# Scores per head on 32 array rows, in a three-step round of a gated attention kernel

## The chip, the cores and the metric

One Trainium2 chip, one core. The metric is the device time of one execution in microseconds (us). Engines are named as the profile names them: PE is TensorE (matrix products, with PEld for its weight loads), DVE is VectorE, ACT is ScalarE, POOL is GpSimd, SP is SyncE, which here only issues transfers.

## The reference

Eight sequences of 512 tokens with 256 features go through a gated linear attention against a context and then through a mixture of experts. The part around the change, for one sequence, with 8 heads of 32 features:

```python
qk = jnp.einsum('hsd,htd->hst', qh, kh) / np.sqrt(DH)
C = qk * D_mat                                   # D_mat = exp(log_D - max), causal
normalizer = jnp.maximum(jnp.abs(C.sum(axis=-1, keepdims=True)), jnp.exp(-max_log_D))
h = jnp.einsum('hst,htd->hsd', C / (normalizer + EPS), vh)
```

`q` is the layer-normed token, `k` and `v` are both the context. After a layer norm and a residual, each token goes through 2 shared experts (hidden 1024) and the best 2 of 8 routed experts, and all is summed.

## The kernel before, in words

The first part of the kernel handles attention, routing and the shared experts; the second, from about 765 us on, handles the routed experts and is not touched.

A sequence is cut in J = 4 blocks of 128 tokens. What lies before a block enters through a `state` (one product of 132 columns for each half of the heads), what lies in it is computed directly, in a round j for each block:

1. exponents: for each half g of the heads (4 heads), a matmul with `identb` and `causal`, and one with `exp_lhs` and `exp_rhs` (56 rows) on top, 512 columns each, into banks 0 and 1;
2. scores: for each half, one fp32 matmul of 512 columns into banks 2 and 3. Its stationary side is the context block, all 128 features of the half; its moving side is `qmask`, which holds the queries four times, each time with all but one head's 32 features at zero (`headmask`). So a contraction over 128 rows gives each head's own product. `qmask` is filled by DVE (g = 0, L698) and POOL (g = 1, L475), four instructions each for a sequence;
3. `decay` = exp of banks 0 and 1 by ACT (L567); `ct` = scores x scale x `decay` by DVE (L767), one instruction for each half;
4. state products into bank 0 (L1066) and value products (L1071), eight fp32 matmuls, each head's beside the next in banks 2 and 3; `hn` by DVE (L775 to L783) adds them up.

An fp32 matmul appears in the trace as two records. banks(b, j) are PSUM banks 0 to 3, except that sequence 0 takes banks 4 to 7 for odd j.

Each engine follows one list of steps written by hand: `START` before the first pass, `FIRST`, then `ORDER` for each pass, `ORDER_6` for the last but one. In pass b, `U` is a unit of the shared experts of sequence b (16 in all: up product, Gelu and cast on ACT, low part on DVE, down product of an earlier unit), digits and S, T, V, W, X are steps of `back(b+1)` (the attention of the next sequence: the digits are its rounds), F, G, M, R, C, c are steps of `front(b+2)` (norm, transposes, gates, the operands of the exponents), A, Q, B, D, E are routing, H hands the tokens over to the shared experts (`xhs` on ACT, `xls` on DVE), L is the last down product and Y the `finish` of sequence b-1, P the base of the output. Each engine does its own share of a step and goes on; between engines there are only semaphores. An engine that waits in one step so holds back all its later ones.

In a pass before, round 0 had no unit between its two steps, rounds 1 to 3 one each, with others between rounds; PE issued exponents and scores together in the first step of a round, and waited for `decay` and `ct` in the second.

## Time and profile before

| | |
|---|---|
| median of 3 runs | 1243.25 us (1241.1 to 1245.12) |
| profiled execution | 1241.27 us, its span 1239.5 us |
| PE busy | 1137.4 us (92%), weight loads 996.7 us |
| DVE busy | 919.4 us (74%) |
| ACT busy | 837.6 us (68%) |
| POOL busy | 341.8 us (28%) |
| mean granted TensorE clock | 0.964 of full speed |

The span runs from the first to the last instruction; the execution's time is 1.8 us more. Busy shares are means over the whole span. PE's matmuls overlap in the records: the distance from one start to the next says what a matmul really costs in a row of them, not its own duration.

### The profile page before, as it was taken

To read this page: it belongs to the slowest core of one execution; us is meant where nothing else is said; L and a number is where in the kernel's file an instruction comes from. 1 tells how busy PE (TensorE), PEld (TensorE's weight loads), DVE (VectorE), ACT (ScalarE), POOL (GpSimd) and SP (SyncE) were. 2 spreads that over 40 slices of the span, in tenths; PEclk is the share of its full clock that TensorE was granted. 3 is DMA by queue.
4 is the path that set the end of the run, shared out by engine and by line. 5 is a ranking of instruction groups with operands and counts; after the bars stand their busy time and mean duration, and the time that the engine had idled before them with its cause. 6 is when DMAs were issued, how large, how long until landed. Compare 5 with 4: busy or idle time off the path is not lost. (4 is left out here: it accounts for less than half of the span.)

```text
span 1239.5 us, 21821 instructions
## 1 busy us (share of the span) xinstructions
PE 1137.4 (92%) x7861; PEld 996.7 (80%) x7861; DVE 919.4 (74%) x2215; ACT 837.6 (68%) x1441; POOL 341.8 (28%) x319
## 2 busy tenths in 40 slices
PE   2748999999989999989989897999999999999996
PEld 1436776886777777777868787999999999999996
DVE  5885696686777777866955564888888888888883
ACT  3526556566476556565664353999999999999994
POOL 7121221510510412313113020233333233333333
PEclk9776999999999999999999898999999999999998
DMA  6110011111010100110001035788888888888872
GB/s 197 34 35 17 34 36 35 36 35 35 35 52 23 65 27 32 46 35 35 19 17 44 1 121 170 219 220 233 239 212 232 244 208 232 244 209 230 246 186 27
DMA packets 141692, 136.17 MB, mean 110 GB/s; under 512 B 48599, under 2 KB 127585, under 8 KB 141585
## 3 DMA queue, kind: packets, MB, share of 16 engines
q1 hardware_dynamic: 122948, 111.68, 28.6%
q0 software_dynamic: 14304, 18.75, 9.2%
q10 hardware_dynamic: 4332, 4.34, 1.0%
q8 instruction: 63, 1.03, 0.3%
q14 instruction: 45, 0.36, 0.1%
HBM read 109.42 MB, written 25.33 MB: 109 GB/s over the span
## 5 line engine op out<-in xcount | busy, mean ns | idle before, releaser
L1358 DVE TENSOR_TENSOR wlo<-big,whi 128x512 fp32r<-128x512 f32 x312 | 219.9, 716 | 21.8 <-ACT whi L1311 14.4
L1311 ACT CAST whi<-big 128x512 fp32r<-128x512 f32 x312 | 191.2, 615 | 6.5 <-PEq L420 5.1
L590 ACT ACTIVATE shared_hraw<-bank,b1s 128x512 f32<-128x512 f32 x128 | 88.1, 688 | 153.9 <-PE bank L1119 153.6
L1283 PE MATMUL bank<-xhi,whi 128*128 128x256 f32 x624 | 175.6, 281 | 6.3 <-DVE xlo L1372 5.1
L1261 PE MATMUL bank<-whi,hhi 128*128 128x256 f32 x624 | 178.1, 285 | 0.0
L1283 PE MATMUL bank<-xhi,wlo 128*128 128x256 f32 x624 | 174.5, 280 | 0.0
L1261 PE MATMUL bank<-wlo,hhi 128*128 128x256 f32 x624 | 174.4, 280 | 0.0
L1261 PE MATMUL bank<-whi,hlo 128*128 128x256 f32 x624 | 174.4, 280 | 0.0
L1283 PE MATMUL bank<-xlo,whi 128*128 128x256 f32 x624 | 174.3, 279 | 0.0
L1333 ACT ACTIVATE hraw<-bank,b 128x256 f32<-128x256 f32 x312 | 147.9, 474 | 36.2 <-PE bank L1283 35.3
L835 DVE TENSOR_TENSOR shared_hlo<-shared_hraw,shared_hhi 128x512 fp32r<-128x512 f32 x128 | 93.1, 731 | 96.4 <-ACT shared_hhi L593 92.9
L495 POOL DMA_INDIRECT sorted_tokens<-rowbuf,slots x64 | 66.7, 1042 | 322.5 <-DVEq L911 305.5
L1102 PE MATMUL bank<-whs,shared_hhi 128*128 128x256 f32 x512 | 150.2, 293 | 3.8 <-DVE shared_hlo L835 3.8
L1402 DVE TENSOR_TENSOR hlo<-hraw,hhi 128x512 fp32r<-128x512 f32 x156 | 108.0, 693 | 55.3 <-ACT hhi L1338 49.7
L1102 PE MATMUL bank<-whs,shared_hlo 128*128 128x256 f32 x512 | 146.0, 285 | 0.0
L1102 PE MATMUL bank<-wls,shared_hhi 128*128 128x256 f32 x512 | 145.9, 285 | 0.0
L1436 POOL DMA_INDIRECT out_dram<-yt,token x78 | 135.4, 1736 | 29.3 <-issue 18.7
L1119 PE MATMUL bank<-xhs,whs 128*128 128x512 f32 x256 | 118.1, 461 | 9.5 <-ACT shared_hraw L590 5.9
L1283 PEld LDWEIGHTS bank<-xhi,whi 128*128 128x128 f32 x624 | 118.9, 190 | 6.7 <-POOL xhi L1425 5.3
L1283 PEld LDWEIGHTS bank<-xlo,whi 128*128 128x128 f32 x624 | 119.0, 191 | 0.0
L1283 PEld LDWEIGHTS bank<-xhi,wlo 128*128 128x128 f32 x624 | 118.2, 189 | 0.0
L1261 PEld LDWEIGHTS bank<-whi,hhi 128*128 128x128 f32 x624 | 117.7, 189 | 0.0
(275 smaller groups left out, 2634.6 us busy)
## 6 DMA issues: line engine op xcount, KB each, us to landing
big<-in_L_ffn_W_r_dram SPq DMA_DIRECT2D x78, 1024.0 KB, 7.4
qcT<-sorted_tokens SPq DMA_DIRECT2D x39, 260.0 KB, 2.9
xb<-in_x_dram SPq DMA_DIRECT2D x8, 512.0 KB, 4.6
cb<-in_ctx_dram SPq DMA_DIRECT2D x8, 512.0 KB, 3.5
xr<-in_x_dram SPq DMA_DIRECT2D x8, 512.0 KB, 3.5
out_dram<-base ACTq DMA_DIRECT2D x8, 512.0 KB, 2.9
sorted_tokens<-chunk SPq DMA_DIRECT2D x9, 260.0 KB, 3.4
out_dram<-yt,token POOLq DMA_INDIRECT x78, 4.0
```

The source lines that it names most:

```text
L495: nc.gpsimd.indirect_dma_start(out=xs_dram, out_offset=bass.IndirectOffsetOnAxis(ap=slots[:, k, j:j + 1], axis=0), in_=rowbuf[:, j, :], in ...
L590: nc.scalar.activation(hraw[:, k % NHB, :], up_bank[k % 2][:, :], ACT.Gelu, bias=b1s[:, k // M, k % M:k % M + 1]).then_inc(gelu_done, 1)
L835: tt(hlo[:, k % NHB, :], hraw[:, k % NHB, :], hhi[:, k % NHB, :].bitcast(fp32), ALU.subtract).then_inc(hlo_ready, 1)
L1102: last = mm(down_bank[j // 2][:, (j % 2) * D:(j % 2 + 1) * D], h[:, k % NHB, j * P:(j + 1) * P], w[:, e, wsl], start=k == 0 and t == 0 and ...
L1119: last = mm(up_bank[k % 2][:, :], w[:, e, wsl], x_[:, c, :], start=c == 0 and t == 0, stop=c == KD - 1 and t == 2)
L1261: last = nc.tensor.matmul(y_bank[i][j * D // 512][:, (j * D) % 512:(j * D) % 512 + D], l[:, h, j * P:(j + 1) * P], w[i][:, wsl], start=m = ...
L1283: last = nc.tensor.matmul(ub[:, 0:T], w[i][:, wsl], x_[i][:, k, :], start=k == 0 and t == 0, stop=k == KD - 1 and t == 2)
L1311: nc.scalar.copy(whi[i][:, psl], raw[i][:, psl]).then_inc(t_whi, 1)
L1333: nc.scalar.activation(hraw[:, m % NHB, :], psum[m % NU][:, 0:T], ACT.Gelu, bias=b1[i][:, m:m + 1]).then_inc(t_gelu, 1)
L1358: nc.vector.tensor_tensor(wlo[i][:, psl], raw[i][:, psl], whi[i][:, psl].bitcast(fp32), ALU.subtract).then_inc(t_wlo, 1)
L1402: nc.vector.tensor_tensor(hlo[:, h - 1:h + 1, :], hraw[:, h - 1:h + 1, :], hhi[:, h - 1:h + 1, :].bitcast(fp32), ALU.subtract).then_inc(t_ ...
L1436: nc.gpsimd.indirect_dma_start(out=out_r, out_offset=bass.IndirectOffsetOnAxis(ap=token[n % NG][:, j:j + 1], axis=0), in_=yt[i][:, j, :], ...
```

## The change

The masks `headmask` and `qmask` go, with their fills on DVE and POOL (an unused tensor `space` keeps the layout). A head's scores are now a matmul of their own: 32 rows of the array, those on which the head's features lie, and 128 columns. Head r of each half writes to bank r, half g to columns g x 128 onwards, so all four banks are used, and the scores overwrite the exponents, which ACT must have read (`decay_ready`). `ct` takes four instructions, one for each bank. State products go to bank 2, value products to bank 3, one head's 99 columns overlapping the next head's, and `hn` adds them in one instruction. Of the exponents, both `causal` matmuls now come before both `exp_lhs` ones. A round has three steps instead of two (exponents; scores; products), and the lists place units between all of them; H comes before round 0. The wait for `counts_read` before round 3 is gone.

```diff
-        START = "f f f f w w w f f w w f f S w w w 0 w w 0 w w 1 w w g 1 w 2 w g 2 3 3 g T T T V V g g V W h g u g u X g".split()
-        FIRST = "S 0 U 0 1 A U 1 F U Q 2 U F 2 B U P 3 U 3 D G M T E U T U T R V U V U V U R U W U X C U c".split()
-        ORDER = "S 0 L H Y 0 U 1 A U 1 F U Q 2 U F 2 B U P 3 U 3 D U G M T E U T U Z T U Z R V U V U V U R U W U X C U c".split()
-        ORDER_6 = "S 0 L H Y 0 U 1 A U 1 U Q 2 U 2 B U P 3 U 3 D U T E U T T U V U V V U W U X U U U U".split()
+        START = "f f f f w w w f f w w f f S w w w 0 w w 0 0 w w 1 w w 1 g 1 w 2 2 w g 2 3 3 3 g T T T V V g g V W h g u g u X g".split()
+        FIRST = "S 0 U 0 U 0 1 A U 1 U 1 2 F U 2 Q U 2 3 F U 3 P U 3 B U D G M T E T U T R V U V U V R U W X C U c".split()
+        ORDER = "S H 0 L 0 Y U 0 1 U 1 A U 1 2 F U 2 Q U 2 3 F U 3 P U 3 B U D G M T E U T U Z T U Z R V U V V U R U W U X C U c".split()
+        ORDER_6 = "S H 0 L 0 Y U 0 1 U 1 A U 1 2 U 2 Q U 2 3 U 3 P U 3 B U D T E U T T U V V V U W U X U U U U".split()
...
-                    for r in range(HG):
-                        last = nc.gpsimd.tensor_scalar(qmask[:, 1, r, :], qcT[:, 1, :], headmask[:, r:r + 1], None,
-                                                       ALU.mult)
-                    last.then_inc(qmask_pool, 1)
...
-                    for r in range(HG):
-                        last = ts(qmask[:, 0, r, :], qcT[:, 0, :], headmask[:, r:r + 1], None, ALU.mult)
-                    last.then_inc(qmask_dve, 1)
...
-                        for g in range(KD):
-                            last = stt(ct[:, g * HG:(g + 1) * HG, :],
-                                       banks(b, j)[2 + g][:, :].rearrange("p (h s) -> p h s", s=P), SCALE,
-                                       decay[:, g * HG:(g + 1) * HG, :], ALU.mult, ALU.mult)
+                        for r in range(HG):
+                            last = stt(ct[:, :, :].rearrange("p (g r) s -> p g r s", r=HG)[:, :, r, :],
+                                       banks(b, j)[r][:, 0:KD * P].rearrange("p (g s) -> p g s", s=P), SCALE,
+                                       decay[:, :, :].rearrange("p (g r) s -> p g r s", r=HG)[:, :, r, :], ALU.mult, ALU.mult)
...
+                    def exponents(j):
                         cj = slice(j * P, (j + 1) * P)
-                        if b > 0 and j > 0:
-                            pe.wait_ge(hn_ready, J * b + j)
                         if b == 0 and j > 1:
                             pe.wait_ge(hn_ready, j - 1)
-                        if j == 3 and b > 0:
-                            pe.wait_ge(counts_read, b)
-
                         for g in range(KD):
                             mm(banks(b, j)[g][:, :], identb[:, :], causal[:, :].unsqueeze(1).to_broadcast([P, HG, P]),
                                start=True, stop=False)
+                        for g in range(KD):
                             last = mm(banks(b, j)[g][:, :], exp_lhs[:, cj],
                                       exp_rhs[:, j, g * HG:(g + 1) * HG, :].rearrange("p h s -> p (h s)"),
                                       start=False, stop=True)
                         last.then_inc(exp_done, 1)
+
+                    def scores(j):
+                        cj = slice(j * P, (j + 1) * P)
+                        pe.wait_ge(decay_ready, J * b + j + 1)
                         if j == 0:
                             pe.wait_ge(state_ready, b + 1)
-                            pe.wait_ge(qmask_dve, b + 1)
-                            pe.wait_ge(qmask_pool, b + 1)
+                        elif b > 0:
+                            pe.wait_ge(hn_ready, J * b + j)
                         for g in range(KD):
-                            last = mm(banks(b, j)[2 + g][:, :], qcT[:, KD + g, cj], qmask[:, g, :, cj], start=True, stop=True)
+                            for r in range(HG):
+                                last = mm(banks(b, j)[r][:, g * P:(g + 1) * P], qcT[r * DH:(r + 1) * DH, KD + g, cj],
+                                          qcT[r * DH:(r + 1) * DH, g, cj], start=True, stop=True)
                         last.then_inc(score_done, 1)
...
+                    for j in range(J):
+                        if j == 0:
+                            pe.wait_ge(lhs_ready, b + 1)
+                            pe.wait_ge(exp_act, b + 1)
...
+                        if b > 0 or j == 0:
+                            exponents(j)
+                        yield
+                        if b == 0 and j + 1 < J:
+                            exponents(j + 1)
+                        scores(j)
                         yield
                         cj = slice(j * P, (j + 1) * P)
-                        pe.wait_ge(decay_ready, J * b + j + 1)
+                        pe.wait_ge(ct_ready, J * b + j + 1)
                         if j > 0:
                             for g in range(KD):
-                                mm(banks(b, j)[0][:, g * HW:(g + 1) * HW], qcT[:, g, cj], state[:, g, j - 1, :],
+                                mm(banks(b, j)[2][:, g * HW:(g + 1) * HW], qcT[:, g, cj], state[:, g, j - 1, :],
                                    start=True, stop=True)
-                        pe.wait_ge(ct_ready, J * b + j + 1)
                         vflat = vaug[:, j, :, :].rearrange("p h e -> p (h e)")
                         for h in range(NH):
-                            last = mm(banks(b, j)[2 + h // HG][:, (h % HG) * PW:(h % HG + 1) * PW], ct[:, h, :],
+                            last = mm(banks(b, j)[3][:, h * VW:h * VW + PW], ct[:, h, :],
                                       vflat[:, h * VW:h * VW + PW], start=True, stop=True)
```

## Rows read from the trace of the kernel before

**Rows 1.** Busy time by stretch: from:to, length, each engine's busy us, clock, DMA
```profile
...
43.20:69.40 26.20, 22.48 (x110) 14.13 (x108) 19.83 (x52) 8.71 (x16) 0.00 (x0) 0.96 0.13 41
...
111.70:151.00 39.30, 38.53 (x227) 28.94 (x226) 24.01 (x74) 21.30 (x28) 5.72 (x6) 1.00 0.08 29
...
196.00:234.40 38.40, 37.51 (x214) 27.48 (x215) 25.12 (x75) 23.35 (x30) 5.79 (x6) 1.00 0.13 43
234.40:282.20 47.80, 45.68 (x283) 38.62 (x280) 38.92 (x102) 29.16 (x43) 14.75 (x14) 0.96 0.10 33
```

**Rows 2.** What TensorE waited for, 110 to 680 us: total, times, longest
```profile
...
PE bank L1037 <- ACT big L555: 11.9, 6, 2.3
PE bank L1119 <- ACT shared_hraw L590: 4.8, 6, 0.8
PE bank L1071 <- DVE chunk L767: 4.0, 6, 0.7
```

**Rows 3.** Timeline of PE, round 1 of a pass: start us, us, instruction
```profile
...
203.96 0.39 PE L1037 MATMUL bank<-causal,identb 128*128 128x512 bf16 x1
...
205.25 1.99 PE L1048 MATMUL bank<-big,qcT 128*128 128x512 f32 x4
...
207.30 0.39 PE L1119 MATMUL bank<-xls,whs 128*128 128x512 f32 x1
207.53 0.39 PE L1119 MATMUL bank<-xhs,wls 128*128 128x512 f32 x1
```

**Rows 4.** Timeline of PE, end of round 2: state and value products
```profile
...
220.45 0.61 PE L1066 MATMUL bank<-state,qcT 128*128 128x132 f32 x4
220.90 1.92 PE L1071 MATMUL bank<-vaug,chunk 128*128 128x99 f32 x16
222.66 0.18 PE L1135 MATMUL bank<-sel,tri 128*128 128x32 bf16 x1
```

**Rows 5.** Timeline of PE: the first matmuls of two units in succession
```profile
...
244.21 0.40 PE L1119 MATMUL bank<-xhs,whs 128*128 128x512 f32 x1
...
247.04 0.40 PE L1119 MATMUL bank<-xhs,whs 128*128 128x512 f32 x1
```

**Rows 6.** Timeline of ACT at the start of a pass
```profile
...
195.85 1.28 ACT L567 ACT_TABLE_LOAD   x1
197.34 1.09 ACT L567 ACTIVATE chunk<-bank 128x512 f32<-128x512 f32 x2 [0.21 <-PE bank L1039]
198.32 1.05 ACT L629 CAST xhs<-unT 128x1024 fp32r<-128x1024 f32 x1
202.91 0.40 ACTq L597 DMA_DIRECT2D out_dram<-base  x1
...
204.63 0.69 ACT L590 ACTIVATE shared_hraw<-bank,b1s 128x512 f32<-128x512 f32 x1
205.35 0.62 ACT L593 CAST shared_hhi<-shared_hraw 128x512 fp32r<-128x512 f32 x1
```

**Rows 7.** Timeline of DVE: qmask beside POOL idle, ct, finish, qmask beside POOL
```profile
...
88.31 1.67 DVE L698 TENSOR_SCALAR big<-qcT,headmask 128x512 f32<-128x512 f32 x4
...
199.26 1.29 DVE L767 SCALAR_TENSOR_TENSOR chunk<-bank,chunk 128x512 f32<-128x512 f32 x2 [3.54 <-PE bank L1048]
...
201.60 1.28 DVE L842 TENSOR_TENSOR base<-base,bank 128x512 f32<-128x512 f32 x2
...
240.25 2.90 DVE L698 TENSOR_SCALAR big<-qcT,headmask 128x512 f32<-128x512 f32 x4 [1.90 <-ACT qcT L529]
```

**Rows 8.** Timeline of POOL: its half of qmask
```profile
...
73.88 6.29 POOL L475 TENSOR_SCALAR big<-qcT,headmask 128x512 f32<-128x512 f32 x4
```

**Rows 9.** Timeline of PE: a pass's first exponents, last products, next pass's exponents
```profile
...
195.97 0.38 PE L1037 MATMUL bank<-causal,identb 128*128 128x512 bf16 x1 [1.34 <-ACT big L555]
...
232.48 1.92 PE L1071 MATMUL bank<-vaug,chunk 128*128 128x99 f32 x16
...
282.24 0.38 PE L1037 MATMUL bank<-causal,identb 128*128 128x512 bf16 x1 [1.36 <-ACT big L555]
```

More of the change, by code:

```diff
@@ L116, in xattn_moe_kernel @@
         take_two = A("take_two", [KE, 1])
-        headmask = A("headmask", [P, HG])
+        A("space", [P, HG])
         blockmask = A("blockmask", [P, HG, VW])
@@ L144, in xattn_moe_kernel @@
         qn = A("qn", [P, J, D])
-        qmask = big[0][:, :].rearrange("p (g r s) -> p g r s", g=KD, r=HG)
         norm_x, norm_u = ((A(f"bn6_{n}", [P, J, 6]), A(f"mv_{n}", [P, J, 2]), A(f"nw_{n}", [P, 5, J])) for n in "xu")
@@ L240, in _ @@
                 nc.gpsimd.memset(causal[:, :], 0.0)
-                nc.gpsimd.memset(headmask[:, :], 1.0)
                 nc.gpsimd.memset(exp_lhs[:, :], 0.0)
@@ L763, in back @@
                     for j in range(J):
+                        yield
                         dve.wait_ge(score_done, J * b + j + 1)
                         dve.wait_ge(decay_ready, J * b + j + 1)
-                        for g in range(KD):
-                            last = stt(ct[:, g * HG:(g + 1) * HG, :],
-                                       banks(b, j)[2 + g][:, :].rearrange("p (h s) -> p h s", s=P), SCALE,
-                                       decay[:, g * HG:(g + 1) * HG, :], ALU.mult, ALU.mult)
+                        for r in range(HG):
+                            last = stt(ct[:, :, :].rearrange("p (g r) s -> p g r s", r=HG)[:, :, r, :],
+                                       banks(b, j)[r][:, 0:KD * P].rearrange("p (g s) -> p g s", s=P), SCALE,
+                                       decay[:, :, :].rearrange("p (g r) s -> p g r s", r=HG)[:, :, r, :], ALU.mult, ALU.mult)
                         last.then_inc(ct_ready, 1)
@@ L772, in back @@
                         dve.wait_ge(pv_done, J * b + j + 1)
+                        pvv = banks(b, j)[3][:, 0:NH * VW].rearrange("p (h e) -> p h e", e=VW)
                         if j > 0:
                             rr = eexp[:, NW + (j - 1) * NH:NW + j * NH].unsqueeze(2).to_broadcast([P, NH, VW])
-                            own.done(tt(hn[:, j, :, :], banks(b, j)[0][:, 0:NH * VW].rearrange("p (h e) -> p h e", e=VW),
+                            own.done(tt(hn[:, j, :, :], banks(b, j)[2][:, 0:NH * VW].rearrange("p (h e) -> p h e", e=VW),
                                         rr, ALU.mult))
-                        for g in range(KD):
-                            pvv = banks(b, j)[2 + g][:, 0:HG * PW].rearrange("p (h e) -> p h e", e=PW)[:, :, 0:VW]
-                            dst = hn[:, j, g * HG:(g + 1) * HG, :]
-                            if j > 0:
-                                last = tt(dst, dst, pvv, ALU.add)
-                            else:
-                                last = nc.vector.tensor_copy(dst, pvv)
-                        last.then_inc(hn_ready, 1)
+                            tt(hn[:, j, :, :], hn[:, j, :, :], pvv, ALU.add).then_inc(hn_ready, 1)
+                        else:
+                            nc.vector.tensor_copy(hn[:, j, :, :], pvv).then_inc(hn_ready, 1)
                         yield
@@ L1026, in back @@
                     yield
-                    def scores(j):
+                    def exponents(j):
                         cj = slice(j * P, (j + 1) * P)
-                        if b > 0 and j > 0:
-                            pe.wait_ge(hn_ready, J * b + j)
                         if b == 0 and j > 1:
                             pe.wait_ge(hn_ready, j - 1)
-                        if j == 3 and b > 0:
-                            pe.wait_ge(counts_read, b)
                         for g in range(KD):
@@ L1052, in back @@
-                    pe.wait_ge(exp_act, b + 1)
-                    if b == 0:
-                        pe.wait_ge(s_const, 6)
-                        scores(0)
-                    for j in range(J):
-                        if b > 0:
-                            scores(j)
-                        elif j + 1 < J:
-                            scores(j + 1)
+                    for j in range(J):
+                        if j == 0:
+                            pe.wait_ge(lhs_ready, b + 1)
+                            pe.wait_ge(exp_act, b + 1)
+                            if b == 0:
+                                pe.wait_ge(s_const, 6)
+                        if b > 0 or j == 0:
+                            exponents(j)
+                        yield
+                        if b == 0 and j + 1 < J:
+                            exponents(j + 1)
+                        scores(j)
```

6 lines of the change are left out of this document (removed).

## The prediction

> **What bounds the kernel now.** I read the page first: TensorE is busy for 92% of the span, but a busy PE is not a PE at its peak, so I went on to the busy time by stretch. From 680 us on (the last pass and the routed experts) no changed instruction runs. The change lives in seven stretches of rounds that run beside units of the shared experts, and in one without units (43.2 to 69.4). In the pass that begins at 196 PE is busy 37.5 of 38.4 us over the rounds and 45.7 of 47.8 us over the rest, while DVE is busy 25.1 and 38.9, ACT 23.4 and 29.2 [rows 1]. The waits confirm it: between 110 and 680 PE waits for ACT's `exp_rhs` 11.9 us in all, then for two things of 4.8 and 4.0 us [rows 2]. So a pass is a queue of PE work in a written order. A microsecond taken off PE is a microsecond won, unless what PE waits for next comes later than that. Both halves of this sentence must be priced.
>
> **PE work of a round, before.** From the first exponent matmul to the scores are 1.29 us: four matmuls of 512 columns at 0.32 each, though 512 columns of a unit's matmul pass in 0.23 (207.30 to 207.53) [rows 3]. The difference, 0.09, comes with each change between 128 and 56 rows. The scores start at 205.25, and the unit behind them reaches its pace of 0.23 at 207.30, so its first matmul really ran from 207.07: the scores cost 1.82. State products cost 0.45 (220.45 to 220.90), value products 1.76 (to 222.66) for sixteen records, 0.11 each [rows 4]. A whole unit is 2.83, from 244.21 to 247.04 [rows 5].
>
> **The same, after.** Exponents: two `causal` matmuls together, then two `exp_lhs`: two changes of rows instead of four, 2 x 0.23 + 2 x 0.32 = 1.10, so 0.19 saved. State and value products keep their shapes, banks apart. The scores become 8 fp32 matmuls of 128 columns, 16 records, with as many columns in all as now (2 x 512). The trace has no four matmuls on different array rows, so this is the unknown price. *Upper bound*: no overlap, each record as long as one of the value products, which also load 128 weight columns: 16 x 0.11 = 1.76, with 0.18 for going to 32 rows and back 1.94. *Lower bound*: four at once, 0.44 + 0.18 = 0.62. I take a value between: matmuls start in order and the second record of a head must wait for its own first, but the next head's first can run beside it, so 9 steps of 0.11 + 0.18 = 1.17, or 0.65 saved. I lean to overlap because the records sit on disjoint rows and write four different banks.
>
> The Trainium skill ("TensorE: Matmul & The Clock Gate", Part 3) gives a measured 3.07 times for four row tiles of 512 columns; by it the scores would cost 1.76 / 3.07 + 0.18 = 0.75, an estimate. Its section on LDWEIGHTS says the opposite for loads: their time goes with the columns, not the rows, which would hold all 16 loads at full price; the value products' 0.11 at only 99 moving columns agree [rows 4]. By that the scores would be 1.94. No row here decides between them.
>
> **DVE, POOL, ACT.** DVE loses `qmask` (2.90 us per sequence beside POOL's own) [rows 7]. `ct` goes from two instructions (1.29 the pair [rows 7]) to four of half the size; I put 1.45 for the four, 0.15 more for the additional starts. `hn` adds once instead of twice, a hair less. POOL loses 6.29 us of `qmask` [rows 8]. None of this is on PE's path where PE bounds; it only gives slack. Once it counts: from 70 to 88 PE waits for DVE (the chain up to the tokens' transposes), POOL's `qmask` runs from 73.9 to 80.2, and DVE's own took 2.90 beside POOL against 1.67 without [rows 7, 8]. I put 1.5 us for that.
>
> **The new dependence.** Scores now overwrite the exponents' banks, so they wait for ACT's `decay` of the same round; before they ran right behind the exponents. The order puts a unit (2.83) between. Walk one pass, with T the start of exponents 0:
> - Exponents end at T+1.1, the late unit (1.4) at 2.5. ACT first copies `xhs` (1.05, now ahead), loads its table (1.28) and does two exponentials (1.09) [rows 6]; it is free at about T-0.1, so `decay` 0 is there at 3.2. PE waits 0.7; scores 3.2 to 4.4; unit 0 (no down part) to 5.8; `ct` 0 ready 6.1; value products to 7.9; exponents 1 to 9.0; unit 1 to 10.4.
> - Now ACT is late. It waits for `finish` on DVE, which sits behind `ct` 0 (1.28 more [rows 7]: 7.4), issues a DMA (0.4), loads the Gelu table (1.28), does Gelu and the cast (1.3 [rows 6]): 10.4. Only then table and `decay` 1: 12.8. PE stands still for 2.4 us. Behind the waiting scores are unit 2 and everything else on PE. Before, the same `decay` 1 delay was covered by a unit whose work came behind the already issued scores, and cost 0.7 (the L1071 wait, [rows 2]).
> - Scores to 14.0; unit 2 to 16.8. `ct` 1 stands in DVE's queue behind the low part of unit 1, whose Gelu stands behind `decay` 1 and two table loads: 17.5, so PE waits 0.9. Value products to 19.9.
> - Rounds 2 and 3: each exponents 1.1, unit 2.83, scores 1.17, unit 2.83, products 2.2 = 10.1, without waits: `decay` needs 1.1 after its exponents, `ct` comes 1.8 to 2.9 after the scores, even behind a front step of DVE. End at T+40.0.
>
> Before, with T at 195.97, round 3's products began at 232.48 and ended 1.76 later, T+38.3, with six units done [rows 9]; after, seven are done. Gain of a pass: 38.3 + 2.83 - 40.0 = 1.1. The rest of the pass loses one unit of PE work and stays PE's: DVE's chain there sheds `qmask` and one low part, 3.6 together, more than the 2.83 PE sheds. The last piece (rows, exponents' operands, the 2 us wait for `exp_rhs`) is the same chain and stays. Six such passes: 6.6 us.
>
> The first pass (111.7 to 151.0 over its rounds [rows 1], six units there) has no `finish`, `late` or `xhs` ahead: no 2.4 us stall. After: 4 x 1.10 + 4 x 1.17 + 4 x 1.76 + 3 x 0.45 + 8 x 2.83 = 40.1 against 39.3 with two units (5.66) fewer: 4.9 gained. Two units leave its second part, where DVE then comes close to PE; I keep 3.5.
>
> The rounds without units (43.2 to 69.4 [rows 1]): `ct` j, `decay` j+1, scores j+1, `ct` j+1 becomes one chain, some 1.2 us longer a round than the old one without scores in it, but a round takes 6.6 now and DVE's front step lies there anyway; I put +1.7 and cancel it with POOL's relief (-1.5).
>
> **Sum.** 1239.5 - 6.6 - 3.5 = 1229.4 us of span; the profiled execution took 1241.3, 1.8 more than its span, and the median of the runs is 1243.25, 2.0 above that. So 1233.
>
> **Rivals.**
> - *Row tiles don't overlap* (scores 1.94). Per pass, T+42.2 instead of 40.0: 1.1 slower than before; six passes +6.6; the first gains 1.8; the rounds without units +3 on their chain. Sum +8: 1251, slower. For it: weight loads set the pace of the value products. Against: disjoint rows. It decides from a score price of about 1.7. Chance 0.22.
> - *The stall does not appear or something covers it, PE stays the bound*: 28 rounds x (0.65 + 0.19) = 23.5, with 1 to 2 of the old waits: 1218. For it: PE's largest waits sum to 21 us in 570 [rows 2]. Against: ACT's order is strict and each piece of it is in the rows. Chance 0.15.
> - *Overlap works but waits eat all*: A is now apart from `decay`, so ACT reloads tables twice more a pass (2.6 us); if that reaches PE once in a pass, the 1.1 is gone and only the first pass is left, 1240 to 1244. Chance 0.13.
> - Forecast, 1226 to 1239: 0.50.
>
> What a measurement can tell from no change is 0.3%, 3.7 us. Faster 0.65, same 0.13, slower 0.22. For 8 in 10 the range takes in most of both outer rivals, with 1 to 2 us beyond their values, since each is itself a sum of bounds: 1216 to 1253.
>
> **What would show it.** After: from the first score matmul to the unit's pace about 1.2 us (1.9 if serial); exponents 1.1; PE waits of some 2.4 us before round 1's scores on ACT's `decay`, in six passes; round 3's products done 40 us after exponents 0; passes of 85 instead of 86.3 us (195.97 to 282.24 [rows 9]). The forecast is wrong if scores cost over 1.7, or if rounds 2 and 3 wait for `ct`, or if the second part of a pass doesn't shorten by a unit.

## The result, and the profile after

| | before | after |
|---|---|---|
| median | 1243.05 us (1241.10 to 1245.12, 4 runs) | 1261.72 us (1256.77 to 1262.06, 4 runs) |
| span of the profiled execution | 1239.5 us | 1259.9 us |
| mean granted TensorE clock | 0.964 | 0.935 |

The ratio is 1.0141 (95% interval 1.0111 to 1.0171): slower by 18.7 us. I had forecast 1233, with 1216 to 1253. Both the sign and the range are missed.

The head of the page of the changed kernel (its span, then busy us, share and instructions of each engine):

```profile
span 1259.9 us, 22586 instructions
...
PE 1126.2 (89%) x8245; PEld 1007.5 (80%) x8245; DVE 895.7 (71%) x2215; ACT 853.8 (68%) x1453; POOL 287.0 (23%) x284
```

PE, DVE and POOL all do less than before, as they were to, and yet the span is 20.4 us longer. So the question isn't what the new instructions cost but where engines stand. Busy time and granted clock by stretch of the changed kernel (columns as in [rows 1]: the first rounds; the first pass's rounds; the rounds and the rest of a later pass):

```profile
41.40:78.80 37.40, 28.44 (x159) 21.15 (x157) 20.49 (x57) 8.83 (x16) 0.00 (x0) 0.55 0.10 29
117.30:156.40 39.10, 39.10 (x301) 32.52 (x300) 24.47 (x76) 24.98 (x33) 0.00 (x0) 1.00 0.05 15
288.60:328.10 39.50, 36.89 (x279) 29.83 (x279) 24.98 (x77) 27.39 (x34) 0.00 (x0) 0.96 0.07 25
328.10:376.20 48.10, 43.41 (x270) 36.46 (x268) 35.87 (x101) 27.92 (x41) 13.62 (x15) 0.96 0.14 47
```

Against [rows 1]: the first rounds took 26.2 us and take 37.4, at a clock of 0.55 where it was 0.96. The rounds of a pass take about as long as they did, with a unit more in them. The rest of a pass takes 48.1 where it took 47.8, though it has a unit less: PE is busy 43.4 us there instead of 45.7, and idle 4.7 instead of 2.1.

I cut both traces at each pass's first exponent matmul, at the end of its last value product, and at the first matmul of the routed experts (all in us; "half clock" is the time that the granted clock was at its lower level, 1.2 GHz, from the first rounds' start to the first pass, and from there to the end of the last rounds). "Last" is the last pass that has rounds; its rest, up to the routed part, also holds the pass of the last sequence, which has none:

| | first rounds | rest | rounds, pass 1 / 2 to 6 / last | rest, pass 1 / 2 to 6 / last | routed part starts | half clock, first rounds / passes |
|---|---|---|---|---|---|---|
| before | 26.4 | 42.1 | 39.3 / 38.4 to 39.8 / 39.3 | 44.9 / 47.8 / 103.2 | 771.1 | 34.3 / 13.7 |
| after | 37.4 | 38.5 | 39.3 / 39.1 to 40.3 / 39.3 | 44.7 / 48.2 / 111.1 | 791.8 | 58.8 / 48.0 |

So the 20.4 us are: 5.6 up to the start of pass 1 (111.7 to 117.3), -0.2 in pass 1, 7.3 in the five later ones (432.7 us became 440.0), 7.9 in the rest of the last pass, and -0.2 in the routed part.

What PE waited for from 100 to 700 us in the changed kernel (columns as in [rows 2]):

```profile
PE bank L1033 <- ACT chunk L556: 14.0, 9, 2.1
PE bank L1016 <- ACT big L544: 9.8, 6, 2.3
PE bank L991 <- DVE rows L701: 8.8, 7, 1.8
PE bank L1106 <- ACT shared_hraw L580: 4.8, 6, 0.8
PE bank L974 <- ACT frow L596: 4.5, 6, 0.8
```

The first row is the forecast stall: scores that wait for `decay`. The third is not in [rows 2] and not in the forecast: the transposes of `rows`, right behind the gates' part, wait for DVE. Both are seen in the timeline. PE of the changed kernel, the start of a pass:

```profile
288.64 0.59 PE L1016 MATMUL bank<-causal,identb 128*128 128x512 bf16 x2 [1.89 <-ACT big L544]
289.17 0.60 PE L1019 MATMUL bank<-big,exp_lhs 56*128 56x512 bf16 x2
...
291.88 0.73 PE L1033 MATMUL bank<-qcT 32*128 32x128 f32 x16 [0.49 <-ACT chunk L556]
292.54 0.50 PE L1106 MATMUL bank<-xhs,whs 128*128 128x512 f32 x1
292.88 0.39 PE L1106 MATMUL bank<-xls,whs 128*128 128x512 f32 x1
293.11 0.39 PE L1106 MATMUL bank<-xhs,wls 128*128 128x512 f32 x1
...
296.01 0.59 PE L1016 MATMUL bank<-causal,identb 128*128 128x512 bf16 x2
296.54 0.60 PE L1019 MATMUL bank<-big,exp_lhs 56*128 56x512 bf16 x2
297.07 0.50 PE L1106 MATMUL bank<-xhs,whs 128*128 128x512 f32 x1
...
300.81 0.73 PE L1033 MATMUL bank<-qcT 32*128 32x128 f32 x16 [2.08 <-ACT chunk L556]
301.47 0.52 PE L1106 MATMUL bank<-xhs,whs 128*128 128x512 f32 x1
301.81 0.61 PE L1106 MATMUL bank<-xls,whs 128*128 128x512 f32 x1
302.21 0.63 PE L1106 MATMUL bank<-xhs,wls 128*128 128x512 f32 x1
302.64 0.63 PE L1106 MATMUL bank<-xhs,whs 128*128 128x512 f32 x1
```

Scores take 0.66 (291.88 to 292.54) and the unit behind them starts 0.11 slower than its pace of 0.23 (0.34 to the next): 0.77 in all. The four exponent matmuls take 1.06 (296.01 to 297.07). The stalls are 0.49 and 2.08. Behind the second one the unit's matmuls follow each other at 0.40 to 0.43 instead of 0.23: the granted clock has fallen to its lower level. It does so right behind this stall in four of the six passes that have it, not in the other two.

In the rest of the same pass, PE and DVE of the changed kernel:

```profile
364.83 0.47 PE L991 MATMUL bank<-ident,rows 72*128 72x72 f32 x4 [1.24 <-DVE rows L701]
...
376.18 0.59 PE L1016 MATMUL bank<-causal,identb 128*128 128x512 bf16 x2 [1.90 <-ACT big L544]
```

```profile
335.09 0.21 DVE L773 SCALAR_TENSOR_TENSOR rnorm<-hn 128x32 f32<-128x32 f32 x1 [3.26 <-ACT qcT L518]
```

DVE stands 3.26 us at the wait that `qmask` needed and that nothing needs now (`qcT_ready`). That was my first suspect for the late `rows`; it was the wrong one.

### The profile page after: what moved, and what is told of

It is laid out like the page before. It is cut to its first block and busy times, and to the rows that moved or that the text cites. A ratio compares the mean times of both kernels' runs of the same rounds, so it can differ in the third digit from the quotient of the medians.

```text
span 1259.9 us, 22586 instructions
## 1 busy us (share of the span) xinstructions
PE 1126.2 (89%) x8245; PEld 1007.5 (80%) x8245; DVE 895.7 (71%) x2215; ACT 853.8 (68%) x1453; POOL 287.0 (23%) x284
## 5 line engine op out<-in xcount | busy, mean ns | idle before, releaser
L1345 DVE TENSOR_TENSOR wlo<-big,whi 128x512 fp32r<-128x512 f32 x312 | 219.9, 716 | 26.2 <-ACT whi L1298 14.3
L1089 PE MATMUL bank<-wls,shared_hhi 128*128 128x256 f32 x512 | 150.3, 294 | 0.0
L1089 PE MATMUL bank<-whs,shared_hlo 128*128 128x256 f32 x512 | 150.0, 293 | 0.0
L1423 POOL DMA_INDIRECT out_dram<-yt,token x78 | 135.7, 1739 | 29.2 <-issue 18.7
L1106 PE MATMUL bank<-xhs,whs 128*128 128x512 f32 x256 | 114.9, 449 | 8.4 <-ACT shared_hraw L580 4.8
```

The source lines that it names most:

```text
L1089: last = mm(down_bank[j // 2][:, (j % 2) * D:(j % 2 + 1) * D], h[:, k % NHB, j * P:(j + 1) * P], w[:, e, wsl], start=k == 0 and t == 0 and ...
L1106: last = mm(up_bank[k % 2][:, :], w[:, e, wsl], x_[:, c, :], start=c == 0 and t == 0, stop=c == KD - 1 and t == 2)
L1345: nc.vector.tensor_tensor(wlo[i][:, psl], raw[i][:, psl], whi[i][:, psl].bitcast(fp32), ALU.subtract).then_inc(t_wlo, 1)
L1423: nc.gpsimd.indirect_dma_start(out=out_r, out_offset=bass.IndirectOffsetOnAxis(ap=token[n % NG][:, j:j + 1], axis=0), in_=yt[i][:, j, :], ...
```

## The experiments

Two theories, formed on the two traces. **Lists**: the new matmuls are as cheap as they look, and the time is lost where the lists now let engines wait (first rounds a serial chain, rounds' second stall, `rows`, the last pass's operands), so moving single steps gives it back. **Clock**: matmuls on 32 rows, or many short ones, pull the granted clock down; lists matter little, and only full rows would give the time back.

Each kernel is compared with before on its own chip. In two of the four series before itself took 1254 to 1255 us, on the other two 1241 to 1242, so ratios don't carry from one series to another; across series I compare the stretches of the table above, each from one trace of the kernel. The changed kernel itself ran only beside series 2 and in the first measurement, not on the chips of series 1 and 4.

**Series 1** (before 1254.48 us).

*full_rows*: scores on all 128 rows, 8 records of 256 columns instead of 16 of 128 (the queries are not masked: the attention values are not the reference's; the other work stands).

```diff
-                        for g in range(KD):
-                            for r in range(HG):
-                                last = mm(banks(b, j)[r][:, g * P:(g + 1) * P], qcT[r * DH:(r + 1) * DH, KD + g, cj],
-                                          qcT[r * DH:(r + 1) * DH, g, cj], start=True, stop=True)
+                        for r in range(HG):
+                            last = mm(banks(b, j)[r][:, 0:KD * P], qcT[:, KD + r % KD, cj],
+                                      qcT[:, 0:KD, cj], start=True, stop=True)
```

> The changed kernel with the scores on all 128 rows again: four fp32 matmuls of 256 columns for a round, as many columns in all as before the change, in the same four banks and at the same place of the round. The moving side is the unmasked queries, so the attention values are not the reference's; everything else is. Theory lists (the 32-row scores cost 0.75 us and are a gain; the loss comes from the step lists, which leave DVE and ACT late where PE used to be): scores 1.8 us instead of 0.75, so up to 1 us more in each of 28 rounds, partly in waits that are there anyway: 10 to 28 us slower than the changed kernel, 1272 to 1290. Theory clock (short 32-row matmuls make PE look idle and the granted clock falls, 165 us at half clock against 92 before): half-clock time goes back to about 100 us and the kernel is no slower than the changed one, at or under 1262.

Measured: 1282.99 us, ratio 1.0224 (1.0202 to 1.0247), span 1279.8. The rounds of a pass take 42.1 to 44.4 instead of 39.1 to 40.3. PE at the first scores of a pass:

```profile
294.06 1.99 PE L1032 MATMUL bank<-qcT 128*128 128x256 f32 x8 [0.50 <-ACT chunk L556]
295.70 0.58 PE L1105 MATMUL bank<-xhs,whs 128*128 128x512 f32 x1
```

1.64 us from start to start, with the same number of columns in all: on 32 rows it is 0.66. So row tiles do run beside each other. Nor do full rows keep the clock up in the passes: 51.6 us at the lower level, against 48.0. Only up to the first pass do they (34.2 against 58.8; the first rounds are 31.6 us long instead of 37.4).

*no_qct_wait*: DVE's useless wait taken out.

```diff
-                    dve.wait_ge(qcT_ready, J * b + J)
```

> The changed kernel without the wait of DVE for qcT_ready, which stood ahead of the qmask fills and was left when they went. In the trace DVE stands 3.3 us there in each pass before the normalisation chain, and PE later waits 1.2 us for rows. Theory lists: DVE's chain starts earlier, PE's wait for rows (8.8 us in all) goes: 5 to 9 us faster than the changed kernel, 1253 to 1257. Theory clock: within 2 us of it, since PE's waits there do not decide.

Measured: 1256.43 us, 1.0011 (0.9998 to 1.0024). The rest of pass 1 falls from 44.7 to 42.5; that of the five later ones stays at 48.1 to 48.2. So this wait is not what makes `rows` late there.

*scores_first*: in the first rounds, scores j are issued before exponents j+1.

```diff
+                        scores(j)
                         if b == 0 and j + 1 < J:
                             exponents(j + 1)
-                        scores(j)
```

> The changed kernel, where in the first sequence a round's scores are issued ahead of the next round's exponents instead of behind them. In the trace each of these rounds takes 10.4 us and is one chain (exponents, scores, ct, products, hn, next exponents), at half clock. Theory lists: the exponents (1 us, 1.9 at half clock) leave the chain three times: 3 to 6 us faster, 1256 to 1259, more if the clock then stays up. Theory clock (it falls because of the 32-row matmuls): rounds stay at half clock, 0 to 3 us faster.

Measured: 1255.50 us, 1.0001 (0.9981 to 1.0020). The first rounds take 31.7 instead of 37.4 us; their rest gives 1.7 of it back (40.2), and they began 2.5 us later in this execution, so pass 1 starts at 115.8 instead of 117.3.

*last_list*: the last pass follows the list `ORDER` of the kernel before (here `ORDER_7`), the others the new one.

```diff
-                for step in START if b < 0 else FIRST if b == 0 else ORDER_6 if b == B - 2 else ORDER:
+                for step in START if b < 0 else FIRST if b == 0 else ORDER_6 if b == B - 2 else ORDER_7 if b == B - 1 else ORDER:
```

> The changed kernel, whose last pass (units and routing of the last sequence, no rounds) follows the step list of the kernel before, so that routing comes after 4 units and not after 8. In the trace the loads for the routed experts are issued 18.8 us later than before while the units end 16.1 us later, and PE waits 9.7 us instead of 5.1 for the first routed tile. Theory lists: 4 to 5 us faster than the changed kernel, 1257. Theory clock: no change.

Measured: 1255.84 us, 1.0004 (0.9988 to 1.0020), span 1253.8. The rest of the last pass takes 104.4 instead of 111.1. How much of the 6.7 us is the edit's is not sure: the other kernels with the new list there, among them the changed kernel run again, took 107.6 to 109.9, so it is worth between 3 and 7 us. What DVE waits for there, after and in this kernel:

```profile
788.41 0.69 DVE L1345 TENSOR_TENSOR wlo<-big,whi 128x512 fp32r<-128x512 f32 x1 [7.83 <-DMA gr_col<-in_L_ffn_g_routed_dram]
```

```profile
780.71 0.69 DVE L1346 TENSOR_TENSOR wlo<-big,whi 128x512 fp32r<-128x512 f32 x1 [3.27 <-DMA gr_col<-in_L_ffn_g_routed_dram]
```

And what PE waits for from 600 to 800 us, after:

```profile
PE bank L1270 <- DVE xlo L1359: 9.7, 1, 9.7
PE bank L1067 <- DVE rowbuf L800: 8.8, 1, 8.8
```

Before had 5.1 us in the place of the first row, and so has last_list. The second row is another matter: 8.8 us here, 3.1 before, and 9.3 in last_list. It stands in the rest behind the last rounds, which follows `ORDER_6`, and no edit of mine but late_finish's move of Y touches that list; what makes `rowbuf` late there I haven't tested. In the new list of the last sequence's pass seven units stand ahead of B and eight ahead of D, where there were four and six. So the last pass's routing is done later, and SP, which waits for it, issues the routed experts' loads 126.1 us after the pass's first exponents (767.41) instead of 120.0 (748.61).

**Series 2** (before 1241.03 us).

*changed_again*, the changed kernel unedited. 

> The changed kernel as it is, beside the runs that follow. In the last series the kernel before took 1254 instead of 1243 us, so a ratio is only sure beside the changed kernel on the same chip. Theory lists and theory clock both expect the ratio of the first measurement, 1.014; if the ratio is nearer 1.000, the last series' variants gained nothing and the machine decides about 1%.

Measured: 1260.72 us, 1.0135 (1.0100 to 1.0170): the result stands. Its rounds and middle passes agree with the first trace within 0.3 us; the rest of the last pass took 109.7 instead of 111.1, pass 1 began at 118.2 instead of 117.3, and 51.2 us of the passes were at half clock.

*before_again*, the kernel before unedited. 

> The kernel before as it is, for its profile beside the others. Expected: the passes of 86 us as before (rounds 38.3, rest 48.0), and any added time in the transfers of the routed experts or at the boundary ahead of them, not in the passes.

Measured, one execution: 1241.58 us, span 1239.5.

*three_fixes*: no_qct_wait, scores_first and last_list together. 

> The changed kernel with the three edits together: no wait of DVE for qcT_ready, scores ahead of the next exponents in the first sequence, and the last pass by the step list of before. Theory lists: the gains lie in different stretches and add up: 12 to 17 us faster than the changed kernel in the same series, which is about the kernel before. Theory clock: under 5 us.

Measured: 1249.26 us, 1.0064 (1.0047 to 1.0081). The first rounds 30.1, the rest of pass 1 42.5, that of the last 104.4. The edits add up: 5.1 (pass 1 starts at 112.2 instead of 117.3), 2.2 and 6.7 are 14.0, and the routed part starts 13.8 earlier, at 778.0 instead of 791.8. The medians differ by less, 11.5 us (1260.72 and 1249.26).

*exponents_only*: the kernel before, with only the exponents' order changed (both `causal`, then both `exp_lhs`).

```diff
                         for g in range(KD):
                             mm(banks(b, j)[g][:, :], identb[:, :], causal[:, :].unsqueeze(1).to_broadcast([P, HG, P]),
                                start=True, stop=False)
+                        for g in range(KD):
                             last = mm(banks(b, j)[g][:, :], exp_lhs[:, cj],
```

> The kernel before with one part of the change alone: both causal matmuls of a round ahead of both exp_lhs ones. 0.19 us of PE saved in each of 28 rounds that PE bounds: up to 5 us faster than before, 0.4%; if waits take it back, 0.

Measured: 1241.39 us, 0.9989 (0.9976 to 1.0002): nothing that can be told from no change. The four matmuls take 1.07 us as forecast, and three of the five later passes' rounds are 0.6 us shorter (37.8). But the other two took 39.0 and 40.4, and the routed part starts at 770.8 against 771.1: the gain went to the clock, 27.3 us at the lower level in the passes instead of 13.7 (17.3 in before_again). The other executions bear it out: seven of ten had a mean granted clock of 0.958 or 0.959, where before has 0.962 to 0.966 on this chip, and the three at 0.962 to 0.965 took only 1237.2 to 1237.9 us.

**Series 3** (before 1242.24 us). Here the aim was the five middle passes.

*late_finish*: in the new list, `finish` (Y) goes from ahead of round 0's scores to behind round 1's exponents, so that ACT reaches `decay` 1 before it takes up the output (`ORDER_6` likewise).

```diff
-        ORDER = "S H 0 L 0 Y U 0 1 U 1 A U 1 2 F U 2 Q U 2 3 F U 3 P U 3 B U D G M T E U T U Z T U Z R V U V V U R U W U X C U c".split()
+        ORDER = "S H 0 L 0 U 0 1 Y U 1 A U 1 2 F U 2 Q U 2 3 F U 3 P U 3 B U D G M T E U T U Z T U Z R V U V V U R U W U X C U c".split()
```

> The changed kernel with Y (finish of the last sequence, on which ACT waits before it issues a transfer) behind the first exponents of round 1 instead of ahead of unit 0, in ORDER and ORDER_6. Theory lists: ACT no longer stands behind DVE there, decay 1 is ready before PE wants it, the 2.1 us stall of PE goes and the rounds of a pass fall from 39.4 to about 37.3: 10 to 13 us faster than the changed kernel. Theory clock: half-clock time in the passes (55 us) stays, and at most the 2.1 us themselves are saved; if the clock drops come from this stall, they go too and passes save up to 3 us each.

Measured: 1238.77 us, 0.9970 (0.9960 to 0.9980), span 1235.1. Rounds of the later passes 36.6 us each (the last 37.5) instead of 39.1 to 40.3. What PE waits for, 100 to 700 us:

```profile
PE bank L1067 <- DVE rowbuf L800: 9.3, 1, 9.3
PE bank L991 <- DVE rows L701: 8.8, 7, 1.8
PE bank L1016 <- ACT big L544: 7.3, 6, 1.9
...
PE bank L1054 <- DVE chunk L755: 3.8, 6, 0.7
PE bank L1033 <- ACT chunk L556: 2.5, 5, 0.5
```

`decay` costs 2.5 us in all instead of 14.0; what comes in its place (L1054, the forecast's wait for `ct` 1) is 3.8 (1.9 before the edit). This edit of one letter is worth 24.9 us of the routed part's start (791.8 to 766.9): 16.1 in the five middle passes, 5.1 in the last, and 3.6 ahead of pass 1, where nothing was edited. Those 3.6 are chance: the first rounds took 32.3 us in this execution and 37.4 to 37.7 in the six others with the same code there.

*unit_behind_gates*: one unit moved from between B and D, ahead of the gates, to the Vs behind them.

```diff
-        ORDER = "S H 0 L 0 Y U 0 1 U 1 A U 1 2 F U 2 Q U 2 3 F U 3 P U 3 B U D G M T E U T U Z T U Z R V U V V U R U W U X C U c".split()
+        ORDER = "S H 0 L 0 Y U 0 1 U 1 A U 1 2 F U 2 Q U 2 3 F U 3 P U 3 B D G M T E U T U Z T U Z R V U V U V U R U W U X C U c".split()
```

> The changed kernel with one unit of ORDER moved from between B and D to behind the gates (R V U V U V U R). In the trace PE does 4 units between the gates and the rows, before it did 5, and waits 1.2 us there for rows, whose chain (gates, ACT's logarithm and tables, Gelus, DVE's low parts and scans) starts at the gates. Theory lists: the unit fills that wait, 1 to 1.5 us of each of five passes: 5 to 7 us faster. If instead DVE is late for another reason, the wait stays and nothing changes.

Measured: 1264.08 us, 1.0166 (1.0147 to 1.0184), not faster as I expected but 3.4 us above the changed kernel on the same chip. The rest of a later pass takes 47.4 to 49.1, once 52.2, instead of 48.2. The wait for `rows` is gone from the five passes, a new one is there (PE, 100 to 700 us):

```profile
PE bank L1033 <- ACT chunk L556: 14.1, 10, 2.1
PE bank L1016 <- ACT big L544: 10.3, 6, 2.3
PE bank L1133 <- DVEq L887: 5.8, 5, 1.2
```

The unit between B and D had covered DVE's part of the routing; without it D's transposes wait 1.2 us in each of five passes.

*all_lists*: three_fixes, late_finish and unit_behind_gates together. 

> The changed kernel with all edits so far: no wait for qcT_ready, scores ahead of the next exponents in the first sequence, the last pass by the list of before, Y behind exponents 1, and the unit behind the gates. Theory lists: the three earlier edits gave 11.5 us, the other two give 15 more: 1232 to 1238 where before is 1241, faster than both kernels. Theory clock: no faster than 1245.

Measured: 1235.49 us, 0.9946 (0.9930 to 0.9961). Rounds 36.6 (once 37.5), first rounds 30.3, last rest 106.0.

*first_full_rows*: the full-row scores of full_rows in the first rounds alone (there the values are not the reference's).

```diff
-                        for g in range(KD):
+                        for g in range(KD if b > 0 else 0):
...
+                        for r in range(HG if b == 0 else 0):
+                            last = mm(banks(b, j)[r][:, 0:KD * P], qcT[:, KD + r % KD, cj],
+                                      qcT[:, 0:KD, cj], start=True, stop=True)
```

> The changed kernel with scores on all 128 rows for the first sequence only (unmasked queries, so its attention values are not the reference's), all others on 32 rows. Theory clock: with full-row matmuls the clock in the first sequence's rounds stays up longer, as with full rows everywhere (rounds 31.6 instead of 37.4 us, half clock until pass 1 35 us instead of 64): 4 to 6 us faster than the changed kernel although its matmuls are longer. Theory lists alone: 2 to 4 us slower than it, since the chain of a round grows by 1 us.

Measured: 1256.84 us, 1.0111 (1.0094 to 1.0129). First rounds 31.4 instead of 37.4, their rest 40.2 instead of 38.5, half-clock time up to pass 1 34.1 instead of 58.8 us.

**Series 4** (before 1254.80 us).

*unit_from_ahead*: late_finish, and one unit moved from the stretch just behind G M T E (ahead of the `rows`' transposes) to the Vs; the units from B to E stay.

```diff
-        ORDER = "S H 0 L 0 Y U 0 1 U 1 A U 1 2 F U 2 Q U 2 3 F U 3 P U 3 B U D G M T E U T U Z T U Z R V U V V U R U W U X C U c".split()
+        ORDER = "S H 0 L 0 U 0 1 Y U 1 A U 1 2 F U 2 Q U 2 3 F U 3 P U 3 B U D G M T E T U Z T U Z R V U V U V U R U W U X C U c".split()
```

> late_finish, and in ORDER a unit moved from ahead of the gates (T U Z) to behind them (R V U V U V U R); B U D stays. If the chain that sets the rest begins at the gates, PE reaches the gates 2.8 us earlier, the chain (gates to rows, 16.5 us) starts earlier, and the wait for rows (1.2 us) goes: rest 48.2 to about 47, five passes, 5 to 6 us faster than late_finish. If it begins at the last round (DVE's normalisation), the wait for rows moves or grows and nothing is gained.

Measured: 1233.52 us, 0.9832 (0.9811 to 0.9852). The rest of each later pass 46.5 to 46.6 instead of 48.2, and PE's waits from 100 to 700 us are

```profile
PE bank L1016 <- ACT big L544: 10.3, 6, 2.3
PE bank L1067 <- DVE rowbuf L800: 9.3, 1, 9.3
PE bank L1106 <- ACT shared_hraw L580: 4.8, 6, 0.8
PE bank L974 <- ACT frow L596: 4.5, 6, 0.8
PE bank L1054 <- DVE chunk L755: 3.9, 6, 0.8
...
PE bank L991 <- DVE rows L701: 2.7, 2, 1.8
```

so PE no longer waits for `rows` in the middle passes. Half-clock time in the passes is 20.5 us, with all scores on 32 rows; before has 13.7.

*four_edits*: three_fixes and late_finish. 

> The changed kernel with no wait for qcT_ready, scores ahead of the next exponents in the first sequence, the last pass by the list of before, and Y behind exponents 1 (no unit moved). If the edits add up: the three took 11.5 us off and Y 22, of which some 4 are the first sequence's clock, so 1229 to 1233 where before is 1242.

Measured: 1232.27 us, 0.9825 (0.9803 to 0.9847). Routed part from 761.6.

*five_edits*: four_edits and the unit's move of unit_from_ahead. 

> four_edits with the unit of unit_from_ahead. Chain from the gates: another 5 us off, 1225 to 1228. Chain from the last round: as four_edits.

Measured: 1222.47 us (1221.14 to 1228.66), 0.9755 (0.9731 to 0.9779), span 1219.5; also 19 to 21 us, 1.5 to 1.7%, below the 1241 to 1243 of before on the other chips. The smaller figure is the safer one, since before is 12 us slower on this chip and I don't know why. Either way it beats both kernels. Beside four_edits, on the same chip, it shows what the unit's move is worth: 9.8 us, the rest of the five passes going from 48.1 to 46.2.

*before_late_finish*: the kernel before, with Y moved from ahead of round 0's second step to behind round 1's first (`ORDER_6` likewise).

```diff
-        ORDER = "S 0 L H Y 0 U 1 A U 1 F U Q 2 U F 2 B U P 3 U 3 D U G M T E U T U Z T U Z R V U V U V U R U W U X C U c".split()
+        ORDER = "S 0 L H 0 U 1 Y A U 1 F U Q 2 U F 2 B U P 3 U 3 D U G M T E U T U Z T U Z R V U V U V U R U W U X C U c".split()
```

> The kernel before with Y moved behind the scores of round 1. If ACT's wait for finish costs there too, the wait of PE for ct in round 1 (0.7 us in five passes) goes: 3 to 5 us faster than before, ratio 0.996 to 0.998. If the changed list alone made it harmful: no change.

Measured: 1264.58 us, 1.0089 (1.0063 to 1.0115): slower. PE's waits, 100 to 700 us:

```profile
PE bank L1037 <- ACT big L555: 13.8, 6, 2.3
PE bank L1037 <- DVE hn L781: 8.7, 6, 1.5
PE bank L1102 <- DVE shared_hlo L835: 6.9, 6, 1.6
```

In the trace of before the last two are 0.6 us (once) and 3.8 us (twice, `shared_hlo` being its fourth row). So in the old list `finish` behind round 1's start seems to hold up `hn` and the low part of the unit on DVE, and the gain of late_finish to belong to the three-step round, in which a unit stands ahead of what needs them. The ratio, taken on one chip, shows that the edit does not help there. The reason is argued only: I have no trace of before on this chip, and the trace of this kernel is also longer where nothing was edited (the rest of pass 1 takes 47.4 instead of 44.9, with PE idle for 3.27 us ahead of L990 and nothing in the profile that it waits for).

## Why the prediction was wrong, by its steps

**The prices of the instructions: right, and better than forecast.** Exponents 1.06 (forecast 1.10), `ct` 1.41 (forecast 1.45):

```profile
46.11 1.41 DVE L755 SCALAR_TENSOR_TENSOR chunk<-bank,chunk 128x256 f32<-128x256 f32 x4
```

Scores were forecast at 1.17, between 0.62 and 1.94, and took 0.77. So the mechanism, overlap, was right, and its size was underrated: the chain of 9 steps that the forecast assumed isn't there. The Trainium skill ("TensorE: Matmul & The Clock Gate", Part 3) gave 3.07 times for four row tiles, by which I had worked out 0.75 as an estimate: the trace agrees within 0.02, although these matmuls have 128 columns and load weights for each. My reading of the Trainium skill's section on LDWEIGHTS (same page), by which the 16 loads would stay at full price, is not borne out. Part 3 in the Trainium skill says also that loads overlap matmuls on other row groups; 0.041 us a record, each with a load of its own, agrees with that. The rival "row tiles don't overlap" falls with it: full_rows shows what scores at 1.64 cost, 3 to 5 us more in the rounds of a pass.

**The walk through a pass's rounds: the waits right, the total in part by luck.** Forecast T+40.0 with stalls of 0.7 and 2.4 and a wait of 0.9 for `ct` 1; measured 39.1 to 40.3 with 0.49, 2.08 to 2.12, and 0.96 in two passes. The scores were forecast too dear by 0.40 a round, 1.6 a pass, and something not in the sum made up for it. In five of the six passes that is in part the clock, at its lower level for 3.4 to 6.8 us of the rounds. Pass 2 has none of this and still takes 39.1, so about 0.7 stay open. late_finish takes the stall out, and the rounds of the five middle passes fall by 2.5 to 3.7 us: by 2.5 in pass 2 (2.4 less idle time, no clock in it), by more where the clock had been down. Half-clock time in the passes goes from 48.0 to 37.6 us, and to 20.5 with `rows` on time as well.

**"The rest of the pass loses one unit of PE work and stays PE's": wrong, and the step on which the gain in the middle passes hung.** It loses the unit (2.83) and is 0.3 to 0.4 longer. PE's idle time there grows by as much as 2.5 us (5.9 against 3.4 in passes 4 and 5, both without a fall of the clock): 1.23 for `rows`, 0.76 for ACT's copy `frow` right behind D, and 0.5 more for POOL. For the first: with one unit fewer from the round's end to `rows`, the chain of ACT and DVE work that starts at the gates and ends in `rows` has less to hide behind. I had compared sums (DVE sheds 3.6, PE 2.83) and not asked at which point the chain starts: what DVE sheds lies ahead of the gates, what PE sheds lies beside the chain. Shown by unit_from_ahead, which beside late_finish's edit changes only where the unit stands: 48.2 to 46.6, where late_finish alone left 48.2, and the wait gone. That the useless `qcT_ready` wait was the cause fell with no_qct_wait; it is worth 2.2 us in pass 1 alone. What in the chain (ACT's tables and Gelus, or DVE's scans) is the longest part I haven't separated. Even then the rest is only 1.2 us shorter than before, of a unit's 2.83. The wait for `frow` (L974, 0.76 in each pass) is still there: before had a unit between D and G that covered it, the new list has none, and in before's pass 1, whose list had D G too, it was 0.82. Some 0.5 more is routing: step B now stands behind the last round instead of among the rounds, so its matmuls, and D's all, fall into the rest. No run moves either.

**"I put +1.7 and cancel it with POOL's relief": wrong in size.** The first rounds take 11.0 us more, of which their rest gives back 3.6 and the time ahead of them 1.8; 5.6 remain. PE in two of those rounds, after:

```profile
53.77 1.24 PE L1033 MATMUL bank<-qcT 32*128 32x128 f32 x16
56.54 1.25 PE L1054 MATMUL bank<-state,qcT 128*128 128x132 f32 x4 [1.54 <-DVE chunk L755]
57.58 3.57 PE L1058 MATMUL bank<-vaug,chunk 128*128 128x99 f32 x16
...
62.21 1.04 PE L1016 MATMUL bank<-causal,identb 128*128 128x512 bf16 x2 [1.06 <-DVE hn L766]
```

The chain is one link longer than I drew it: scores j are issued behind exponents j+1, and those wait for `hn` j-1, so `hn`, exponents, scores, `ct` and products run one behind the other, and PE runs them all at the lower clock (value products 3.57 instead of 1.92). Two edits that have nothing in common, another order (scores_first, 31.7) and longer matmuls on full rows (first_full_rows, 31.4), both bring back almost 6 us; and the unedited code took 32.3 once. So in the traces of kernels with the new step order this stretch takes either 30.0 to 32.3 or 37.4 to 37.7 us, and small things decide which. That length and clock feed each other is my reading; what exactly tips it stays open. Nor is all of it won for the end: in those two kernels the stretch began 2 us later and its rest was longer, so pass 1 started only 1.5 and 2.5 us earlier; with the other list edits (three_fixes) it was 5.1.

**"From 680 us on no changed instruction runs": wrong.** No new instruction, but a new list. The rest of the last pass was never priced and cost 7.9 us (6.5 when the kernel was run again), in the first trace the largest single part. last_list gives back 3 to 7 of it, and where it does, the wait for the first routed tile falls from 9.7 to 5.1. The wait for `rowbuf` in that stretch (8.8 against 3.1) stays, so part of the cause is open. I read the diff's lists for their rounds only, and not for what is issued behind one more unit.

**The sum.** Forecast -10.1 of span, measured +20.4, 30.5 apart. By stretches: up to pass 1 5.6 (forecast 0), pass 1 3.3 (forecast -3.5, came -0.2: its rounds take 39.3 with two units more, as forecast or better, but the rest with two fewer is only 0.2 shorter, of which DVE's useless wait explains 2.2; the rest of that is open), the five middle passes 12.8 (forecast 5 x -1.1, came +7.3), the last with its rest 9.0 (forecast -1.1, came +7.9), less 0.2 in the routed part. Of the rivals, "waits eat all" comes nearest, but its waits were to take a few us, not 20, and it placed them at ACT's tables. **Of the two theories**, the lists hold: five edits of lists and waits, none of them touching a matmul, turn +1.4% into -2.5% on that chip, and into -1.5 to -1.7% against before on the others. The clock is part of it, but mostly as a follower: the time at half clock goes when the stalls go (48.0, 37.6, 20.5), while full rows leave it at 51.6. A stall alone does not decide it, though: the stall of 2.08 was followed by a fall in four passes of six, and of the four waits of 2.3 for `exp_rhs` at pass starts of before, two were.

## What to carry to other kernels

Price moved work at both ends: what it covered where it stood, as much as what it costs where it goes. For each engine's chain ask at which instruction it starts, since work shed ahead of that instruction does not shorten it. A diff of step lists changes every stretch that follows the list, also those in which none of its new instructions runs; and a wait should leave together with the work that needed it.

## What the runs showed of the hardware

- Sixteen fp32 records of 128 columns, each with its own 32-row weights, in turn on four groups of rows and into four banks, take 0.66 us, 0.041 each; eight of 256 columns on all rows take 1.64 us.
- A stall of PE of 2.08 us was followed at once by matmuls at half the pace (0.43 instead of 0.23 each) in four passes of six. Taking the stall out gave 2.5 us in a pass where the clock had stayed up, and up to 3.7 where it had been down for 6.8 us. Shortening PE's work also went with a lower clock: with exponents_only PE did 0.2 us less a round, and half-clock time in the passes was 27.3 us, against 13.7 and 17.3 in the two traces of before.
- The kernel before takes 1241 to 1243 us on some chips and 1254 to 1255 on two others, at a mean granted clock of 0.958 to 0.965, about as elsewhere (0.962 to 0.966). I have no profile of it there and don't know why. The kernels with the new list don't show it: in the middle passes their rounds and rests on those chips agree with those on the others within 0.3 us where the code and the clock are the same.
